# A recurrent attention and gated feed-forward block on one Trainium2 core: its front rebuilt around a token-major first norm, one scan per batch and weight units half as large

## The reference

```
k  = layernorm(x);  v = ctx
# along the 256 tokens of each batch, per channel, w = -exp(time_decay), u = time_first:
y_t = (sum_{s<t} exp(w*(t-1-s) + k_s) v_s + exp(u + k_t) v_t) / (the same sums without v)
x  = x + tanh(g_xattn) * y
h  = silu(layernorm(x) @ W1.T) * (layernorm(x) @ W3.T)
out = x + tanh(g_ffn) * (fwht(h) @ W2.T)      # fwht: Walsh-Hadamard transform over H
```

## Time and profile before

| | us |
|---|---|
| median of 3 runs | 1183.73 (1183.5 to 1184.18) |
| the profiled execution | 1183.45 |
| its span, first to last instruction | 1181.6 |
| TensorE busy | 1088.4 (92%) |
| VectorE busy | 724.6 (61%) |
| GpSimd busy | 485.3 (41%) |
| ScalarE busy | 227.5 (19%) |

### The profile page before, as it was taken

How to read it: one execution, slowest core, us unless ns; L and a number is a source line. 1 busy time by engine, 2 the same in 40 slices (tenths; PEclk the granted TensorE clock), 3 DMA queues, 4 the chain that set the end, 5 groups by cost and what they waited for, 6 DMA issues and landing times.

```text
span 1181.6 us, 13867 instructions
## 1 busy us (share of the span) xinstructions
PE 1088.4 (92%) x5263; PEld 547.9 (46%) x5344; DVE 724.6 (61%) x812; ACT 227.5 (19%) x308; POOL 485.3 (41%) x405
## 2 busy tenths in 40 slices
PE   6586886879999999999999999999999999999998
PEld 3255765654444444444444444444444444444443
DVE  5778768664883469556874479465975479342112
ACT  4345123011201230112201230113102130110000
POOL 1626434632554427533643427433643445421111
PEclk8789898889999999999999999999999999999999
DMA  9703200100001000100001000100010000000000
GB/s 355 288 1 121 93 1 1 72 1 36 1 1 72 1 36 1 72 2 36 1 19 53 14 24 1 72 2 36 1 72 1 37 1 1 1 1 36 1 1 36
DMA packets 10772, 47.21 MB, mean 40 GB/s; under 512 B 1232, under 2 KB 3408, under 8 KB 5968
## 3 DMA queue, kind: packets, MB, share of 16 engines
q1 hardware_dynamic: 10704, 46.28, 10.2%
HBM read 33.69 MB, written 12.58 MB: 39 GB/s over the span
## 4 chain that ended last, share of the span: by engine, by line
PE 78%; DVE 10%; POOL 4%; issue 4%; ACT 2%; DMA 2%; SPq 0%; DVEq 0%; POOLq 0%; ACTq 0%
PE po L385 9%; PE pg L375 9%; PE po L383 9%; PE pg L373 8%; PE pl L375 8%; PE po L384 8%; PE pg L374 8%; PE pl L373 8%; PE pl L374 7%; DVE v L620 2%; PE pst L349 2%; POOL bv L804 1%; DVE newton_tmp L585 1%; DVE newton_tmp L587 1%; PE po L363 1%
## 5 line engine op out<-in xcount | busy, mean ns | idle before, releaser
L818 POOL TENSOR_TENSOR work<-work 128x512 bf16<-128x512 f32 (+1 forms) x144 | 180.9, 1259 | 454.7 <-DVE work L655 454.7
L647 DVE TENSOR_TENSOR work<-work,pl 128x512 f32<-128x512 f32 (+1 forms) x144 | 89.4, 621 | 364.8 <-PE pl L375 320.6
L383 PE MATMUL po<-work,w 128*128 128x512 f16 (+1 forms) x568 | 206.8, 364 | 38.9 <-POOL work L818 24.6
L373 PE MATMUL pg<-xn,w1h 128*128 128x512 f16 (+1 forms) x576 | 208.5, 362 | 15.4 <-DVE xn L639 7.2
L479 ACT ACTIVATE work<-pg 128x512 f32<-128x512 f32 (+1 forms) x144 | 79.0, 549 | 727.1 <-PE pg L375 726.3
L375 PE MATMUL pg<-xn,w1l 128*128 128x512 f16 (+1 forms) x576 | 208.0, 361 | 1.6 <-issue 0.2
L385 PE MATMUL po<-work,w 128*128 128x512 f16 (+1 forms) x568 | 207.1, 365 | 1.5
L375 PE MATMUL pl<-xn,w3l 128*128 128x512 f16 (+1 forms) x576 | 204.9, 356 | 1.3
L373 PE MATMUL pl<-xn,w3h 128*128 128x512 f16 (+1 forms) x576 | 205.3, 356 | 0.0
L374 PE MATMUL pg<-xn,w1h 128*128 128x512 bf16 (+1 forms) x548 | 197.4, 360 | 0.0
L384 PE MATMUL po<-work,w 128*128 128x512 bf16 (+1 forms) x540 | 196.4, 364 | 0.0
(11 more groups left out here) (81 smaller groups left out, 1131.9 us busy)
## 6 DMA issues: line engine op xcount, KB each, us to landing
xin<-x_t SPq DMA_DIRECT2D x7, 1024.0 KB, 4.8
v<-ctx_t SPq DMA_DIRECT2D x7, 1024.0 KB, 6.9
out_t<-x SPq DMA_DIRECT2D x7, 1024.0 KB, 3.9
w_turn<-w SPq DMA_DIRECT2D x4, 1024.0 KB, 10.0
x<-w_t SPq DMA_DIRECT2D x3, 1024.0 KB, 4.8
xn<-w_t SPq DMA_DIRECT2D x3, 1024.0 KB, 4.8
work<-w_t SPq DMA_DIRECT2D x2, 1024.0 KB, 12.6
xin<-x_t SPq DMA_DIRECT2D x2, 512.0 KB, 10.3
```

The costliest lines, as they stand in the source:

```text
L373: pe.matmul(bank[:, 0:run.n], hi, nh, start=(k == 0), stop=False)
L383: pe.matmul(acc, w2h[:, j, d * P:d * P + P], h, start=first, stop=False, skip_group_check=True)
L647: dve.tensor_tensor(hf[:, j % 2, run.cols], sg[:, j % 2, 0:run.n], pl[:, j % 2, 0:run.n], ALU.mult).then_inc(hidden, 1)
L818: pool.tensor_tensor(hl[:, j % HBUF, run.cols], hf[:, j % 2, run.cols], hh[:, j % HBUF, run.cols], ALU.subtract).then_inc(hid_lo, 1)
```

## The change

- **First norm.** x is loaded a second time, token-major (`xt`, in the buffer of the numerators). VectorE takes mean and variance of each token's 512 channels (`bn_stats`, `bn_aggr`) and runs the reciprocal root on one number per token (`tok_moments_of`); ScalarE scales and shifts each token block (`tok_normalise`); TensorE transposes 128x128 blocks into the statistics bank in rounds (`transposes`), and ScalarE takes both exponentials of each round out of that bank (`exps`). Two of the four statistics go, with their centring, squares, sums, root and scaling.
- **Scans.** Buffers are batch-major with one leading zero per row, so one scan of 1028 elements does a batch's 4 channel tiles. The states are added on VectorE, 1024 elements at a time (`add_states`). VectorE's reciprocal stays, in two parts of a slot each (`recip0`, `recip1`); the quotients are one GpSimd operation per batch.
- **Second norm.** In half runs the variance is taken per token (8 matmuls with one column), its root runs on two columns, and `spread_half` broadcasts it.
- **Weights.** W1 and W3 come in 16 units of 512 KB; each is cast on ScalarE and limited and split on VectorE (`unit_lo`), as the last step of the slot that `unit_slot` names; TensorE waits for units at every even slot of run 0.
- **Order.** The front's steps stand in three tables of slots, for TensorE with a place in the slot (0 after the gate product, 1 after lin, 2 at the end). `hidden_hi(j)` follows `times_lin(j)` at once; in half runs both come ahead of the front's steps of the slot. The order of the first transfers and of VectorE's work ahead of run 0 changes.

Of the diff, cut to its core:

```diff
-NEWTON_FIRST = 2
...
-WP = 4
...
+WP = 8
 PW = H // WP
+UNITS = 2 * WP
...
-STAT_STEP = [(0, 1), (2, 0), (11, 1), (13, 0)]
-FRONT1_AT = (0, 0, 1, 2, 4, 4, 5, 6, 6, 7, 8, 9, 9, 10, 11, 11)
-FRONT2_AT = (12, 13, 15, 16, 18, 19, 20, 22, 23, 24, 25, 27, 28, 29, 30, 31)
-SPLIT_SLOT = {1: 2, 2: 3, 3: 4, 5: 5, 6: 6, 8: 7}
-LO_ON_VECTOR = (3, 5, 7)
...
+FULL_AT = dict(tok=0, exps=((1, 0), (1, 2), (2, 0), (2, 2)), weigh=3, scan_b=4, scan_a=5, add=6, recip0=7, recip1=8,
+               quot=8, resid=9, sum_mean=10, mean=(11, 1), centre=11, sum_var=12, var=(13, 0),
+               rsqrt=13, spread=None, norm=14)
+HALF1_AT = dict(tok=0, exps=((1, 2), (2, 2)), weigh=3, scan_b=4, scan_a=5, add=6, recip0=7, recip1=8,
+                quot=8, resid=10, sum_mean=None, mean=(10, 2), centre=11, sum_var=None, var=(11, 2),
+                rsqrt=12, spread=(12, 2), norm=13)
+FULL2_AT = dict(tok=15, exps=((17, 0), (17, 2), (18, 0), (18, 2)), weigh=19, scan_b=20, scan_a=21, add=22, recip0=23,
+                recip1=24, quot=24, resid=26, sum_mean=26, mean=(27, 2), centre=28, sum_var=28,
+                var=(29, 2), rsqrt=30, spread=None, norm=31)
...
+        unit_slot = {n - 2: n for n in range(4, UNITS)}
+        unit_slot.update({0: 2, 1: 3})
...
+            load_half_tokens(0)
...
+                load_rows(g)
+            load_half_v(0)
+            load_half_x(0)
+            load_unit(0)
+            load_unit(1)
+            put_rows(0)
+            put_rows(1)
+            load_unit(2)
+            load_unit(3)
+            put_rows(2)
+            put_rows(3)
             sp.wait_ge(put, 16 * GROUPS)
             for g in range(GROUPS):
                 turn_rows(g)
...
+            load_half_tokens(1)
+            load_half_v(1)
+            load_half_x(1)
+            for n in range(4, UNITS):
+                load_unit(n)
...
+            def transposes(run, m):
+                wait(pe, tok_normed, run.done * JB)
+                if run.half and run.r == 0:
+                    bank, per = pl[:, m, :], 2
+                else:
+                    bank, per = pst[:, :], 2 if run.half else 1
+                    if m == 0:
+                        pe.wait_ge(normed, run.before)
                     else:
...
+                        pe.wait_ge(exp_b, run.nth(m * per - 1, KT))
+                for i in range(per):
+                    k = m * per + i
+                    for n, blk in enumerate(run.blocks):
+                        col = i * T + n * P
+                        mm = pe.transpose(bank[:, col:col + P], xt[:, blk, k * P:(k + 1) * P], ident)
+                mm.then_inc(transposed, 1)
...
+            def mean_half(run):
+                pe.wait_ge(x1_done, run.done)
+                pe.wait_ge(exp_b, run.nth(KT - 1, KT))
+                for k in range(KT):
+                    mm = pe.matmul(pst[:, 0:T], ones[:, :], x1[:, 0, k, run.cols], start=(k == 0),
+                                   stop=(k == KT - 1))
+                mm.then_inc(stat_mean, 1)
+            def var_half(run):
+                pe.wait_ge(squared, run.nth(0, 1))
+                pe.wait_ge(centred, run.done)
+                for j in range(JB):
+                    for k in range(KT):
+                        mm = pe.matmul(pst[:, T + j:T + j + 1], batch_rows(ea, run.r)[:, k, j * P:(j + 1) * P],
+                                       ones[:, 0:1], start=(k == 0), stop=(k == KT - 1))
+                mm.then_inc(stat_var, 1)
+            def spread_half(run):
+                pe.wait_ge(newton, run.nth(0, 1) * LN_STEPS)
+                for j in range(JB):
+                    mm = pe.matmul(pst[:, j * P:(j + 1) * P], spread[:, 1, j:j + 1].to_broadcast([P, P]), ident,
+                                   start=True, stop=True)
+                mm.then_inc(stat_spread, 1)
...
+                            pe.wait_ge(raw_lo, 2 * (j * P // PW) + 2)
...
+            def tok_normalise(run):
+                act.wait_ge(tok_chain, run.nth(0, 1) * TOK_STEPS)
+                for blk in run.blocks:
+                    act.activation(xt[:, blk, :], xt[:, blk, :], ACT.Identity, bias=tiny[:, 3, blk:blk + 1],
+                                   scale=tiny[:, 1, blk:blk + 1]).then_inc(tok_normed, 1)
...
+                    for ahead in at(run, j, "tok", front):
+                        tok_normalise(ahead)
+                    for ahead, m, _ in rounds_at(run, j, front):
+                        exps(ahead, m)
+                    for ahead in at(run, j, "centre", front):
+                        squares(ahead)
+                    for ahead in at(run, j, "norm", front):
+                        norm_hi(ahead)
+                    if run.half and run.r == 0 and j in unit_slot:
+                        unit_hi(unit_slot[j])
...
+            def tok_moments_of(run):
+                if run.half:
+                    dve.wait_ge(xt_half[run.r], 16)
                 else:
...
+                    dve.wait_ge(xt_loaded, run.r * 16 - 16)
+                for blk in run.blocks:
+                    dve.bn_stats(out=parts6[:, blk, :], in_=xt[:, blk, :]).then_inc(tok_part, 1)
+                dve.wait_ge(tok_part, run.done * JB)
+                dve.memset(holder[:, :], 0.0)
+                for blk in run.blocks:
+                    dve.bn_aggr(out=moments[:, blk, :], in_=parts6[:, blk, :]).then_inc(tok_moments, 1)
+                sel = slice(run.blocks[0], run.blocks[-1] + 1)
+                ve, rs, nt, nm = (tiny[:, i, sel] for i in range(4))
+                base = run.r * TOK_STEPS
+                dve.wait_ge(tok_moments, run.done * JB)
+                dve.tensor_scalar(ve, moments[:, sel, 1], EPS, None, ALU.add).then_inc(tok_chain, 1)
+                rsqrt_steps(tok_chain, base, ve, rs, nt)
+                dve.wait_ge(tok_chain, base + LN_STEPS)
+                dve.scalar_tensor_tensor(out=nm, in0=moments[:, sel, 0], scalar=-1.0, in1=rs,
+                                         op0=ALU.mult, op1=ALU.mult).then_inc(tok_chain, 1)
...
+                    seq = buf[:, b * KT:(b + 1) * KT, :].rearrange("p k t -> p (k t)")
+                    dve.tensor_tensor_scan(seq, decays[:, :, :].rearrange("p k t -> p (k t)"), seq, 0.0,
+                                           ALU.mult, ALU.add).then_inc(done, 1)
+            def add_states(run):
+                for i, b in enumerate(run.batches):
+                    dve.wait_ge(scan_b, run.before + (i + 1))
+                    dve.tensor_tensor(batch_rows(eb, b), batch_rows(eb, b), batch_states(ea, b),
+                                      ALU.add).then_inc(den_done, 1)
+                for i, b in enumerate(run.batches):
+                    dve.wait_ge(scan_a, run.before + (i + 1))
+                    dve.tensor_tensor(batch_rows(bv, b), batch_rows(bv, b), batch_states(v, b),
+                                      ALU.add).then_inc(num_done, 1)
+            def reciprocals(run, part):
+                for i, b in enumerate(run.batches):
+                    dve.wait_ge(den_done, run.before + (i + 1))
+                    r = slice(b * KT + part * 2, b * KT + part * 2 + 2)
+                    dve.reciprocal(eb[:, r, :], eb[:, r, :]).then_inc(inv_done, 1)
...
+            def unit_lo(n):
                 dve.wait_ge(raw_hi, n + 1)
                 dve.tensor_scalar(hi_of(n), hi_of(n), F16_MAX, -F16_MAX, ALU.min,
                                   ALU.max).then_inc(raw_clamped, 1)
+                dve.wait_ge(raw_clamped, n + 1)
+                dve.tensor_tensor(lo_of(n), raw[n % 4], hi_of(n), ALU.subtract).then_inc(raw_lo, 1)
             def slots_lo(j):
...
+            def early(run, j, front):
+                for ahead in at(run, j, "norm", front):
+                    normalise(ahead)
+                for ahead in at(run, j, "tok", front):
+                    tok_moments_of(ahead)
+                for ahead in at(run, j, "weigh", front):
+                    weigh(ahead)
+                for ahead in at(run, j, "scan_b", front):
+                    scan(ahead, ea, scan_b)
+                for ahead in at(run, j, "scan_a", front):
+                    scan(ahead, v, scan_a)
+                for ahead in at(run, j, "add", front):
+                    add_states(ahead)
+                for ahead in at(run, j, "recip0", front):
+                    reciprocals(ahead, 0)
...
+            def late(run, j, front):
+                for ahead in at(run, j, "resid", front):
+                    residual(ahead)
+                for ahead in at(run, j, "centre", front):
+                    centre(ahead)
+                for ahead in at(run, j, "rsqrt", front):
+                    rsqrt(ahead)
+                for ahead in at(run, j, "norm", front):
+                    norm_lo(ahead)
...
+                    hidden_hi(run, j)
+                    if run.half:
+                        early(run, j, front)
+                    late(run, j, front)
+                    if run.half and run.r == 0 and j in unit_slot:
```

(21 more changed lines are left out.)

653 lines of the change are left out of this document (271 added, 382 removed).

## The result

The changed kernel took **1201.78 us** (median of 4 runs, 1200.0 to 1202.33) against 1183.95 for the kernel before, run beside it: a ratio of 1.0147, 95% interval 1.013 to 1.0165. It is slower by 1.5%. The forecast was 1197, its range 1182 to 1210. The profiled execution took 1202.33 us, its span 1200.5, 18.9 more than before.

The account below looks back on a forecast made before the run. TensorE was busy 1088.4 of 1181.6 us, with losses in half runs, full-run stalls and a DMA-bound start. Terms -10 (start) + 19 (run 0) + 12 (run 1) - 7.9 (full runs) = +13.1 gave 1197 us; range 1182 to 1210.

Parts of the forecast that it names:

- Start: Stretch up to the first up product: DMA and W2's transforms end earlier, 64 us for 74.07, -10 (bounds 60 and 70).
- Run 0: First half run: TensorE waits every second slot for a unit split last in VectorE's list; 113.4 us against 94, +19.
- four slow stretches of 1.8 us: In the first half run, four waits long enough for a 1.2 GHz clock afterwards, about 1.8 us each, 7.2 in all.
- 0.109 us each: Half runs' up and down products on TensorE: each matmul of 256 columns takes 0.109 us, 60.3 us per half run.
- Rival 2: Port lock: GpSimd's low halves delay VectorE's two-input steps in half runs, some 20 x 0.45 = 9 us more, 1206; chance 0.15.
- Run 1: Second half run: token scaling delays silu, quotient before the hidden low half idles TensorE eleven us; 106 against 94, +12.
- Full runs: Six full runs with a front: stall and two statistics go, transposes come; period 129.2 for 130.0, -7.9 (bounds -17 and +14).
- Rival 1: The units are not what holds the first half run: it keeps its 94 us, total 1178; chance 0.15.
- rival 4: Whole kernel: it cancels, halves lose 8 less, total within 0.2% of 1183.7; chance 0.06.
- Rival 3: Transposes dear: two loads and passes each, 0.43 us, 22 us more in full runs, 1219; chance 0.08.
- The last step of the sum: Whole kernel: +13.1 added to the profiled 1183.45, written as 1196.8 and 0.28, giving 1197 us.

## Why the prediction was right

The direction, the place and the mechanism were as argued. That the total came only 4.8 us over the forecast is in part luck: the start and the half runs were 13.8 us worse than forecast and the full runs 8.0 better (5.8 us net on the span).

- **Start**, -10 forecast, -8.2 measured: right.
- **Run 0**, +19 forecast, +28.6 measured. The mechanism held to the slot: lists ending in a unit's subtraction, TensorE released by it before every even slot, gone when the units are split two slots earlier. The size was off. By the table of pairs the slots up to 13 are 15.2 us longer than their lists, and I had allowed 7.2, for four slow stretches of 1.8 us. TensorE ran at 1.2 GHz after all seven waits, and 24 products at that clock let VectorE wait up to 2.6 us longer for the lin product, ahead of the next unit's split; filling three waits took 8 us off. The step "0.109 us each" for products between the waits was taken from stretches without waits. The other part of the 15.2 us is the next point.
- **Rival 2**, the port, had more in it than its 0.15. VectorE's timeline of slots 8 and 9, beside the quotient on GpSimd:

```profile
138.88 3.24 DVE L737 TENSOR_TENSOR w1l<-xn,w1h 128x1024 bf16<-128x1024 f32 x1
...
143.22 1.57 DVE L737 TENSOR_TENSOR w3l<-xn,w3h 128x1024 bf16<-128x1024 f32 x1
```

  An undisturbed one takes 1.23; the two made up 2.4 us of the 4.9 by which slots 8 and 9 are late. Twenty steps of 0.45, as the rival had it, are not there, but in each half run seven or eight steps of VectorE are stretched, by 0.3 to 2.0 us and some 5 us together, each beside a GpSimd operation; about as much in all as the 9 us of the rival, for which my sum had nothing. In run 0 they lie in the lists that TensorE waits for; no run took them away, so what they cost in the total is not shown. GpSimd loses too: beside VectorE's scans its low half takes 2.53 us for 0.67, while the scan keeps its 2.29. The page "SBUF — State Buffer" of the Trainium skill, "SBUF: two separate sides", calls the shared port an exclusive lock that goes to whichever of the two engines' operations starts first. The rows agree: the scan starts at 104.60 and the stretched low half at 104.83, the quotient at 138.64 and the stretched subtraction at 138.88.
- **Run 1**, +12 forecast, +14.4 measured. The quotient's stall (10.76 for 11) and the scaling's (6.2 for 5.2) were both there. But a stall that is seen isn't a stall that can be had: the next step of the same chain, the mean, was due at nearly the same time, and moving the quotient moved the wait. The last wait of the chain, for the norm's low part (9.31 us), was in the forecast only as the end of the list.
- **Full runs**, -7.9 forecast, -15.9 measured. The gap went as argued; the mis-sized term is the transpose, priced at 0.2 by its weight load, which measures 0.11: 1.4 us per run and 8.6 over six.
- **Rival 1** (the units don't hold run 0) and **rival 4** fell with run 0 at 122.55. **Rival 3** (0.43 per transpose) fell by a factor of four.
- The last step of the sum is a slip of the pen: 1183.45 and 13.1 are 1196.55, and 1196.8 has the 0.28 in it already. It is 1197 either way.

What stays open: run 1 at its best still takes 104 to 106 us, with the exponentials, the reciprocals, the statistics and the norm each holding TensorE for some microseconds. No run separated these beyond the reciprocals. How the overshoot of run 0 divides between clock and port, whether one slot more would do for the units where two did, and whether the finer units alone would help the kernel before, was not tried.

## What to carry to other kernels

When a prepared operand is the last entry of a list that the consumer waits for, the length of the list is on the path, however idle its engine is on average; put slots between preparing and using (two more were enough here). To a wait of TensorE of some 5 us add what the products behind it lose at 1.2 GHz, here some 2 us, above all if the releasing engine waits for those products. Before moving a step to remove a wait, look where the next step of the same chain falls due, and read the result by stage, since a total can hide a gain of 12 us and a loss of 9.

## What the runs showed of the hardware that was not expected

- A 128x128 fp32 transpose in a stream of products delays it by 0.106 us (96 more cost 10.2), although its duration in the profile is 0.272.
- Added products made the kernel faster: 48 of 512 columns in three waits raised the granted clock of their stretch from 0.78 to 0.90 and took 8 us off the total.
- Beside a scan of VectorE a GpSimd operation of 0.67 us took 2.53; beside a GpSimd quotient a VectorE subtraction of 1.23 took 3.24. In both cases the one that started some 0.2 us later was the one stretched.
